# First expert network of a two-layer graph kernel: the hidden rows made with the weights held still, from a copy at a fixed place

## The reference

```python
def _moe(tokens, router_w, w1, b1, w2, b2):      # 8 experts, 256 -> 256 -> 256
    logits = tokens @ router_w.T
    probs = softmax(logits)
    rw, re = top_k(probs, 2)
    rw = rw / maximum(rw.sum(-1, keepdims=True), 1e-12)
    combine = zeros((N, 8)).at[arange(N)[:, None], re].set(rw)
    out = tokens
    for e in range(8):
        h = gelu(tokens @ w1[e] + b1[e], approximate=False)
        y = h @ w2[e] + b2[e]
        out = out + combine[:, e:e + 1] * y
    return out
```

## Time and profile before

| | |
|---|---|
| Median of 3 runs | 5789.2 us |
| Lowest and highest | 5780.65 and 5792.94 us |
| The profiled execution | 5784.15 us |
| Its span, first to last instruction | 5782.4 us |
| PE busy | 4086.9 us (71%) |
| DVE busy | 3472.9 us (60%) |
| ACT busy | 2748.9 us (48%) |
| POOL busy | 3350.9 us (58%) |

### The profile page before, as it was taken

The page is one execution under the profiler, slowest core; times in us unless marked ns, Lnnn a source line. Parts: engine busy times, 40 slices in busy tenths (PEclk is TensorE's granted clock), DMA queues, the critical chain, the costliest instruction groups (busy, mean ns, idle before and its releaser), DMA issues.

```text
span 5782.4 us, 74758 instructions
## 1 busy us (share of the span) xinstructions
PE 4086.9 (71%) x17795; PEld 2853.5 (49%) x17795; DVE 3472.9 (60%) x10666; ACT 2748.9 (48%) x5933; POOL 3350.9 (58%) x3492
## 2 busy tenths in 40 slices
PE   1997666766662697868777776655656565797998
PEld 1655554544542585556655555534444444333665
DVE  4367766666677536867888887755555555722111
ACT  0455766666661233578888887522222222243222
POOL 0113777777765744377777777377777777211222
PEclk9998777787785698978988998878777877898999
DMA  3194555555542344244544445344444444210110
GB/s 99 59 261 123 145 139 141 139 139 139 139 111 70 113 123 119 80 132 131 133 132 132 132 132 137 95 132 129 128 129 129 128 128 129 71 43 27 37 32 27
DMA packets 347488, 660.26 MB, mean 114 GB/s; under 512 B 78834, under 2 KB 196608, under 8 KB 346664
## 3 DMA queue, kind: packets, MB, share of 16 engines
q0 software_dynamic: 156336, 433.90, 28.0%
q1 hardware_dynamic: 190732, 221.57, 13.2%
HBM read 541.11 MB, written 115.45 MB: 114 GB/s over the span
## 4 chain that ended last, share of the span: by engine, by line
PE 24%; issue 14%; DVE 12%; POOL 12%; DMA 4%; ACT 3%; DVEq 1%; POOLq 0%; SPq 0%; ACTq 0%
POOL AR L992 8%; PE ps L1216 6%; PE ps L2592 3%; PE ps L2573 3%; DMA AR<-D_z,SRCI 3%; PE ps L2281 3%; PE ps L2069 2%; POOL AR L1670 2%; DVE AR L1106 2%; PE ps L2293 1%; POOL D_sx L1660 1%; DVE AR L1079 1%; DVE AR L1084 1%; PE ps L1178 1%; PE ps L2058 1%
## 5 line engine op out<-in xcount | busy, mean ns | idle before, releaser
L992 POOL DMA_INDIRECT AR<-D_z,SRCI x1856 | 1800.2, 970 | 675.5 <-issue 502.1
L1216 PE MATMUL ps<-AR 128*128 128x264 f32 (+2 forms) x5568 | 1784.1, 475 | 209.9 <-DVE AR L1079 72.4
L1216 PEld LDWEIGHTS ps<-AR 128*128 128x128 f32 x5568 | 1254.3, 236 | 525.0 <-issue 152.7
L992 POOL DMA_INDIRECT AR<-D_h,SRCI x904 | 871.8, 964 | 277.3 <-issue 244.6
L1106 DVE TENSOR_TENSOR AR<-ps,AR 128x264 f32 (+2 forms) x1392 | 588.1, 423 | 163.6 <-DVE AR L1106 128.8
L1263 ACT ACTIVATE AR<-iota_n,NREL 128x128 f32<-128x128 f32 x1856 | 587.2, 389 | 13.2 <-PE ps L1216 10.2
L1084 DVE TENSOR_TENSOR AR<-AR,ps 128x1024 f32<-128x1024 f32 x464 | 558.3, 1203 | 0.0
L1186 PE MATMUL ps<-ident,AR 128*128 128x128 f32 (+2 forms) x174 | 60.2, 346 | 648.5 <-DVE AR L1027 648.5
L1025 DVE TENSOR_TENSOR AR<-AR 128x128 f32<-128x128 f32 (+2 forms) x174 | 49.1, 282 | 781.6 <-SPq L969 779.8
L1280 ACT ACTIVATE AR<-ps 128x128 f32<-128x128 f32 (+2 forms) x174 | 46.5, 267 | 832.4 <-PE ps L1186 827.3
L1276 ACT ACTIVATE AR<-AR,ones 128x1024 bf16<-128x1024 bf16 x348 | 399.5, 1148 | 11.3
(11 more groups left out here) (442 smaller groups left out, 7755.0 us busy)
## 6 DMA issues: line engine op xcount, KB each, us to landing
AR<-D_rel SPq DMA_DIRECT2D x348, 256.0 KB
D_sx<-AR SPq DMA_DIRECT2D x8, 6370.0 KB
AR<-D_z,SRCI POOLq DMA_INDIRECT x1856
AR<-D_h,SRCI POOLq DMA_INDIRECT x928
D_y<-AR SPq DMA_DIRECT2D x106, 128.0 KB, 1.7
AR<-in_L_ffn_Wd SPq DMA_DIRECT2D x8, 1024.0 KB, 12.0
AR<-D_mask SPq DMA_DIRECT2D x58, 128.0 KB
D_h<-AR SPq DMA_DIRECT2D x49, 132.0 KB, 1.7
```

The lines of the kernel that those rows point to most:

```text
L992: e.indirect_dma_start(out=GV[:, u % 48, :], out_offset=None, in_=D_row[L.i], in_offset=bass.IndirectOffsetOnAxis(ap=SRCI[:, u:u + 1], axi ...
L1216: t = e.matmul(banks[n % 3][:, 0:YW], Sr[:, u % 8, :], GV[:, u % 48, L.GW - YW:L.GW], start=(i == 0), stop=(i == 1))
```

## The change

The hidden layer is made in turned form. The stationary operand is now a 128 x 128 piece of the expert's weights, and the moving one is `rxe`, 128 columns wide, so that hidden index comes out on the partitions; that is the form that the output layer wants as its stationary operand. Step 5's turning goes away, and ScalarE's gelu reads `rh0` in SBUF and not PSUM. The stationary pieces are not read from `WA1k` at a register's place: VectorE copies the expert's 2 x 256 columns into `rw1`, a ring of two at fixed places, two slots ahead (`picked`, semaphore `x_w1`). The bias must now differ by partition: `b1T` holds for each expert two columns, loaded by two transfers of single 4-byte elements, and is added repeated along the row.

```diff
-        b1e, b2e = AR.take(2048), AR.take(2048)
+        b1T, b2e = AR.take(2048), AR.take(2048)
...
+        rw1 = AR.ring(2, 2, 256)
...
         def ffn0_sync(e):
             e.dma_start(RW[:, :, :], A["routerT"].rearrange("(k p) n -> p k n", p=128)).then_inc(ffn0_in, 16)
-            e.dma_start(b1e[:, :], A["L0_ffn_b1"].rearrange("e n -> (e n)").partition_broadcast(128)).then_inc(ffn0_in, 16)
+            for m in range(2):
+                e.dma_start(b1T[:, :].rearrange("p (e n) -> p e n", e=8)[:, :, m], A["L0_ffn_b1"][:, 128 * m:128 * m + 128].rearrange("e p -> p e")).then_inc(ffn0_in, 16)
             e.dma_start(b2e[:, :], A["L0_ffn_b2"].rearrange("e n -> (e n)").partition_broadcast(128)).then_inc(ffn0_in, 16)
             e.dma_start(spw[0:1, :], A["pow2"][0:120].unsqueeze(0)).then_inc(ffn0_in, 16)
-            e.wait_ge(ffn0_in, 64)
+            e.wait_ge(ffn0_in, 80)
...
         def ffn0_tensor(e, walk):
...
                     if s >= 2:
                         e.wait_ge(x_hb, s - 1)
-                    w = walk[0].to(s, 256, KW0, 7)
-                    for k in range(2):
-                        t = e.matmul(banks[2 + s % 2][:, 0:256], rxe[s % 3][:, k, :], WA1k[:, k, bass.ds(w, 256)], start=(k == 0), stop=(k == 1))
+                    e.wait_ge(x_w1, s + 1)
+                    for m in range(2):
+                        for k in range(2):
+                            t = e.matmul(banks[2 + s % 2][:, 128 * m:128 * m + 128], rw1[s % 2][:, k, 128 * m:128 * m + 128], rxe[s % 3][:, k, :], start=(k == 0), stop=(k == 1))
                     t.then_inc(x_hps, 1)
...
-                if 2 <= r < NE2 + 2:
-                    s = r - 2
-                    e.wait_ge(x_hb, s + 1)
-                    if s >= 2:
-                        e.wait_ge(x_h, s - 1)
-                    for k in range(2):
-                        t = e.transpose(banks[4 + s % 2][:, 128 * k:128 * k + 128], rh0[s % 3][:, 128 * k:128 * k + 128], ident[:, :])
-                    t.then_inc(x_htr, 1)
...
         def ffn0_scalar(e):
...
-                    e.wait_ge(x_htr, s + 1)
+                    e.wait_ge(x_hb, s + 1)
                     if s >= 3:
                         e.wait_ge(x_ps, s - 2)
-                    e.activation(rhe[s % 3][:, :, :], banks[4 + s % 2][:, 0:256].rearrange("p (k t) -> p k t", k=2), ACT.Gelu).then_inc(x_h, 1)
+                    e.activation(rhe[s % 3][:, :, :], rh0[s % 3][:, :].rearrange("p (m t) -> p m t", m=2), ACT.Gelu).then_inc(x_h, 1)
...
-        def ffn0_vector(e, walk1, walk):
+        def ffn0_vector(e, walk1, walk2, walk):
             route0_vector(e)
             plan0_vector(e)
+
+            def picked(s):
+
+                w = walk1.to(s, 256, KW0, 7)
+                e.tensor_copy(rw1[s % 2][:, :, :], WA1k[:, :, bass.ds(w, 256)]).then_inc(x_w1, 1)
+
+            e.wait_ge(experts_in, 128)
+            picked(0)
+            picked(1)
             for r in range(NE2 + 2):
                 if r < NE2:
-                    w = walk1.to(r, 256, KW0, 7)
+                    w = walk2.to(r, 256, KW0, 7)
                     e.wait_ge(x_hps, r + 1)
                     if r >= 3:
-                        e.wait_ge(x_htr, r - 2)
-                    e.tensor_tensor(rh0[r % 3][:, :], banks[2 + r % 2][:, 0:256], b1e[:, bass.ds(w, 256)], ALU.add).then_inc(x_hb, 1)
+                        e.wait_ge(x_h, r - 2)
+                    bias = b1T[:, bass.ds(w, 2)].unsqueeze(2).to_broadcast([128, 2, 128])
+                    e.tensor_tensor(rh0[r % 3][:, :].rearrange("p (m t) -> p m t", m=2), banks[2 + r % 2][:, 0:256].rearrange("p (m t) -> p m t", m=2), bias, ALU.add).then_inc(x_hb, 1)
+                    if r + 2 < NE2:
+                        picked(r + 2)
```

More of the change, by code:

```diff
@@ L1628, in plan0_vector @@
             e.wait_ge(f_iota, 3)
-            plan0.make(e, rB[NGR % 2][:, 0, :], spw, ffn0_in, 64)
+            plan0.make(e, rB[NGR % 2][:, 0, :], spw, ffn0_in, 80)
             e.tensor_copy(IX0[:, :], plan0.rows[:, :])
@@ L1646, in program @@
         assert end_plan + 8 * 260 <= mark_side
-        x_tr, x_xT, x_hps, x_hb, x_htr, x_h, x_ps, x_taken = [
-            early_sem(n) for n in ("x_tr", "x_xT", "x_hps", "x_hb", "x_htr", "x_h", "x_ps", "x_taken")]
+        x_tr, x_xT, x_hps, x_hb, x_h, x_ps, x_taken, x_w1 = [
+            early_sem(n) for n in ("x_tr", "x_xT", "x_hps", "x_hb", "x_h", "x_ps", "x_taken", "x_w1")]
         y_out = [early_sem(f"y_out{i}") for i in range(8)]
@@ L2651, in _ @@
             join0_vector(e)
-            ffn0_vector(e, Walk(e, "dve1"), walk)
+            ffn0_vector(e, Walk(e, "dve1"), Walk(e, "dve2"), walk)
             mix1a_vector(e)
```

## The result

The changed kernel takes 5764.84 us (median of 5 runs, 5763.94 to 5766.53), the kernel before 5788.19 us (5 runs, 5780.65 to 5792.94). The ratio is 0.9961 with a 95% interval of 0.9947 to 0.9974: **faster by 23 us**, 0.4%. 5766 was forecast.

What follows compares the result with a forecast made beforehand. The prediction took TensorE as the only limit of the steady expert loop. Rounds (20.6 us) plus the loop's end (2.6) gave 23.2 us less: 5789.2 - 23.2 = 5766 us, range 5756 to 5780.

Steps and rivals of the forecast that it cites:

- What bounds the loop: Expert loop: TensorE is the only limit in the steady loop, busy 49.93 of 50 us; a round takes 2.17 us.
- The hidden layer: TensorE in the expert loop: eight records of 128 columns at 0.11 us take 0.88 us, 0.01 more than before.
- The turning: TensorE in the expert loop: the two records that turn the hidden rows go, 0.22 us less per round.
- The round: Expert loop: a steady round falls from 2.17 to 1.96 us; 0.20 less over about 103 rounds gives 20.6 us.
- VectorE: Expert loop: two additions and a copy of 0.42 us take 1.27 us per round, under TensorE's 1.96; cost nothing.
- ScalarE: Expert loop: a gelu of 0.383 to 0.589 us plus a copy stays under 1 us per round; cost nothing.
- SyncE: Loads ahead of routing: two small bias loads replace one of 1 MB; effect 0, bounds -0.6 and +3.9 us.
- The end: End of the expert loop, last hidden layer to last output layer: 2.62 us against 5.20 before, 2.6 us less.
- The start of the loop: First rounds of the expert loop: one turning gained, the wait for the first gelu kept; nothing counted.
- Sum: Whole kernel: 20.6 us in the rounds and 2.6 at the loop's end, 23.2 us less, from 5789.2 to 5766.
- The first rival: TensorE in the expert loop: weight loads set a pace of 0.191 us; round 2.61, kernel 43 us slower, 5832; chance 0.05.
- The third rival: VectorE in the expert loop: each copy waits 0.94 us for a gather; round 2.21 us, kernel 5791; chance 0.03.

Runs made afterwards that it cites:

- experiment 4: Changed kernel with only 64 of the 128 columns moved in each hidden-layer product (result wrong): 5761.42 us, one run; round 1.977 us.
- experiments 1 and 2: Kernel before without the turning of the hidden rows: 5760.47 us, ratio 0.9956; changed kernel with the two turning products put back: 5785.53 us, ratio 1.0004.
- experiment 3: Changed kernel with every copy of the weights made two, three or five times: 5760.83 (one run), 5760.97 and 5804.54 us.

## Why the prediction was right

- **What bounds the loop: right.** TensorE's record starts add up to the round in four kernels: 2.166 before, 1.947 without the turning, 1.977 after, 2.196 with turning put back.
- **The hidden layer: right, 0.01 to 0.02 too small.** 0.88 us was forecast from line 712, 0.89 to 0.90 is what it takes; 0.112 per record and not 0.11. The upper bound of 0.191 was far off: the shown length of a load is not what it costs. Line 1196 of the kernel before (experiment 4) would have given 0.112 ahead of any run.
- **The turning: right**, 0.218 forecast as 0.22; experiments 1 and 2 show it from both sides.
- **The round: right through two small misses.** I forecast 1.96, and took 0.20 less on all rounds, where the terms give 0.21. The steady round is 1.977, 0.189 less. But the kernel before had four longer rounds, which I had not seen in a window of one round, and which are gone: on the mean, 2.180 - 1.978 = 0.202. "It ran ahead of the engine and cost nothing in a steady round" was true of the steady rounds only. Either edit alone, no turning or one walk less, removes them.
- **VectorE: right.** The copy takes 0.427 (0.42 forecast), starts 1.60 us after the hidden layer starts (1.61) and the second addition starts at 2.09 (2.05). "Up to a copy of 1.1 us" is what three copies make, 1.01, and they still hide.
- **ScalarE: right.** 0.408 for the gelu, within its bounds.
- **SyncE: mis-sized.** I took 0 with bounds of -0.6 and +3.9. It is -1.0 to -1.2 at the first product, outside these bounds, and the sign "within a microsecond of 1826" did not come: 1824.57. The step that failed is the issue: 1.23 us each from the earlier trace rows, against 0.47 and 0.58 here. Why it was 1.23 there is not shown; six other loads had been issued in the 3 us before. A second miss took part of that back: from the second bias's issue to the product I put 1.3 + 3 = 4.3 us, and it is 4.99 (its packets start 1.3 us behind the issue and run for 3.3). The net of my own terms was 0.5 us early, which I rounded to 0.
- **The end: a little too large.** 2.62 forecast, 2.94 measured, 2.3 us gained and not 2.6; 0.16 of it is an idle time in front of the last output layer that the trace puts down to no one.
- **The start of the loop: put at nothing.** Its first four rounds take 7.90 us where they took 8.52; one turning fewer ahead of the last hidden layer gives another 0.2.
- **Sum.** 23.2 forecast for the loop, 23.5 measured: 20.4 in the 101 steady rounds, 0.6 in the first four, 2.5 behind the last turning of rows. The start adds 1 us, and the medians show 23.35. That this lies within 0.2 us of the forecast is luck: the interval is 15 to 31 us, the start was left out, and in the loop the missing 0.6 at its beginning makes up for the 0.3 too much at its end.

The first rival, loads that set TensorE's pace, has a true core: experiment 4 shows that the loads do set it. Only they do so at 0.112 us, and 0.136 was where the change would have paid nothing. The Trainium skill (TensorE: Matmul & The Clock Gate, "Back-to-back issue gap") gives 81 against 56 ns for narrow products. That ratio did not hold for fp32 here: 0.112 against the 0.108 of the columns alone. The third rival, copies held up by gathers, fell with experiment 3: three copies, on top of the gathers, left the round where it was, and no copy lost more than about 0.2 us to a gather. No other rival came true either.

## What to carry to other kernels

Where one engine is busy for 50.0 of 50 us, add up the distances between its starts in one round, per kind of record; an edit is then worth the sum before less the sum after, and the other engines count only by whether they stay below that. Find the new kind of record elsewhere in the same trace, and not by its shown length. A product in fp32 may trade a moving operand of 256 columns for two of 128 at nearly no cost, but not for narrower ones: below 128 the weight loads set the pace.

## What the runs showed of the hardware

- Records that each load fresh 128 x 128 fp32 weights start 0.112 us apart at the full clock, whether 64 or 128 columns follow (experiment 4), or one (line 1196 before). The loads are shown as 0.19 us long. With loads of 64 and 16 columns and one moving column the distance is 0.059 and 0.025.
- Copies of 512 fp32 numbers per partition on VectorE, shown as 0.42 us each, start 0.34 us apart when they stand in a row.
- Two loads of 1024 single 4-byte elements were issued in 0.47 and 0.58 us and let the waiting engine go 1.0 to 1.2 us earlier than one broadcast of 1 MB in their place.
- A copy of VectorE that is under way when a gather of GpSimd starts, and ends 0.3 us later, lengthens it from 0.95 to 1.10 us. Copies that only start inside the gather leave it at 0.947 in the middle of 258; one that starts 0.6 to 0.7 us behind its start takes 0.57 us in place of 0.42.
